# A two-layer gated cross-attention model: the first layer's down products in three passes of split operands

## The reference

```
x = x + tanh(g_xattn[0]) * LN(rs * softmax_attention(LN(x), ctx))        # layer 0, 16 heads
x = x + tanh(g_ffn[0]) * ((silu(h @ gate.T * gate_s) * (h @ up.T * up_s)) @ down.T) * down_s
x = x + tanh(g_xattn[1]) * ((linear_attention(q, ctx) * sigmoid(h @ Wg.T + bg)) @ Wo.T)
x = x + tanh(g_ffn[1]) * (top-2 of 16 experts (inner width 352) + one shared expert (704))
```

## Time and profile before

| | |
|---|---|
| median of 3 runs | 962.27 us (962.15 to 965.42) |
| the profiled execution, whole | 964.5 us |
| its span | 962.8 us |
| PE busy | 932.7 us, 97% of the span |
| DVE / ACT / POOL busy | 451.6 / 303.0 / 76.9 us |
| granted TensorE clock, mean | 0.995 |
| layer 0's down products (line 827) | 66.9 us busy |

### The profile page before, as it was taken

One profiled execution on the slowest core, in us unless ns is written; L12 is line 12 of the kernel. 1 busy time (PEld: TensorE's weight loads), 2 busy tenths in 40 slices (PEclk: granted clock), 3 DMA queues, 4 the chain that ended last, 5 costly groups with the idle time before them and its releaser, 6 DMA issues.

```text
span 962.8 us, 17950 instructions
## 1 busy us (share of the span) xinstructions
PE 932.7 (97%) x7523; PEld 720.6 (75%) x7524; DVE 451.6 (47%) x755; ACT 303.0 (31%) x477; POOL 76.9 (8%) x110
## 2 busy tenths in 40 slices
PE   5999999999999999989999999999999999999995
PEld 5878787878788888779999544888798766666554
DVE  6665545455455456873221154597665122222224
ACT  4633333332332334653211121335532222222210
POOL 0000000000000003000000000112006112122210
PEclk9999999999999999999999999999999999999998
DMA  8000010101011012044000300840503449787534
GB/s 338 10 27 34 1 34 1 34 1 34 5 74 34 1 35 78 2 154 175 1 1 1 131 1 0 318 182 1 181 1 131 156 170 329 285 290 241 210 123 166
DMA packets 26773, 96.04 MB, mean 100 GB/s; under 512 B 3282, under 2 KB 4306, under 8 KB 23634
## 3 DMA queue, kind: packets, MB, share of 16 engines
q1 hardware_dynamic: 20354, 72.69, 21.3%
q0 software_dynamic: 6352, 22.35, 6.2%
HBM read 76.37 MB, written 18.66 MB: 99 GB/s over the span
## 4 chain that ended last, share of the span: by engine, by line
PE 88%; DVE 6%; ACT 3%; DMA 2%; issue 1%; SPq 0%; POOL 0%; POOLq 0%; DVEq 0%; ACTq 0%
PE ps L563 18%; PE ps L564 17%; PE ps L565 17%; PE ps L991 10%; PE ps L827 7%; PE ps L1001 5%; PE ps L643 4%; PE ps L626 4%; PE ps L849 1%; PE ps L982 1%; DMA land_c<-in_ctx 1%; PE ps L665 1%; PE ps L963 1%; PE ps L612 1%; PE ps L1008 1%
## 5 line engine op out<-in xcount | busy, mean ns | idle before, releaser
L563 PE MATMUL ps<-arena_r 128*125 128x512 f32 (+1 forms) x416 | 163.8, 394 | 4.2 <-DVE arena_r L1357 4.2
L564 PE MATMUL ps<-arena_r 128*125 128x512 f32 (+1 forms) x416 | 157.0, 377 | 0.0
L565 PE MATMUL ps<-arena_r 128*125 128x512 f32 (+1 forms) x416 | 156.8, 377 | 0.0
L563 PE MATMUL ps<-hT,arena_r 128*128 128x448 f32 (+1 forms) x368 | 136.3, 370 | 2.4 <-DVE arena_r L1376 1.1
L565 PE MATMUL ps<-hT,arena_r 128*128 128x448 f32 (+1 forms) x368 | 134.4, 365 | 0.0
L564 PE MATMUL ps<-hT,arena_r 128*128 128x448 f32 (+1 forms) x368 | 134.4, 365 | 0.0
L991 PE MATMUL ps<-arena 128*128 x336 | 102.9, 459 | 0.0
L1062 ACT ACTIVATE arena<-arena,mbias,mscale 125x448 f32<-125x448 f32 x96 | 66.2, 752 | 102.0 <-DVE arena L1484 101.9
L563 PEld LDWEIGHTS ps<-arena_r 128*125 128x125 f32 (+1 forms) x416 | 78.0, 188 | 21.8 <-DVE arena_r L1357 4.6
L565 PEld LDWEIGHTS ps<-arena_r 128*125 128x125 f32 (+1 forms) x416 | 77.9, 187 | 13.8
L564 PEld LDWEIGHTS ps<-arena_r 128*125 128x125 f32 (+1 forms) x416 | 78.1, 188 | 10.7
(11 more groups left out here) (224 smaller groups left out, 1167.0 us busy)
## 6 DMA issues: line engine op xcount, KB each, us to landing
arena<-in_e SPq DMA_DIRECT2D x16, 1408.0 KB, 6.6
arena<-in_e SPq DMA_DIRECT2D x16, 512.0 KB, 7.4
sorted_rows<-arena POOLq DMA_DIRECT2D x1, 7453.0 KB, 34.0
land_c<-in_ctx SPq DMA_DIRECT2D x8, 752.0 KB, 4.2
arena<-sorted_rows POOLq DMA_DIRECT2D x21, 257.0 KB, 6.1
land_w<-in_gu SPq DMA_DIRECT2D x8, 512.0 KB, 5.3
arena<-token_rows SPq DMA_DIRECT2D x14, 256.0 KB, 4.5
arena<-in_e SPq DMA_DIRECT2D x16, 192.0 KB, 8.8
```

Of the source, the lines that this page charges most:

```text
L563: mm(into, a[0], w[0], start=i == 0, stop=False)
L564: mm(into, a[0], w[1], start=False, stop=False)
L565: last = mm(into, a[1], w[0], start=False, stop=i == len(operands) - 1)
```

## The change

1. **Down products.** `wd0` now lands in its own tensor `land_d` and is split into high and low halves in four pieces; `hidden` writes h in full into the landing area of the gate-up weights of the same m, from where ACT copies the high half and DVE takes the low half in place. `down_of_0` makes three passes, 33 matmuls per tile where there were 11, and waits per chunk for `h_low` and for the weight pieces.
2. **Later weights behind them.** `wg1` and `wo1` need regions that the down products now use: their loads wait for the last down product, `wg1` is split in two pieces between queries 2 to 4 and `wo1` after the attends. `wq1` has another region and waits for the last `hidden`.
3. **Zero fill.** It starts after the last `mix` of layer 0's attention, from a zero row of half the length (twice as many pieces); ACT waits for it ahead of the last layer norm.
4. **The end.** POOL's scatter copies the row numbers before it waits for DVE's copy into `yr`. Tile 6's shared product has no wait for DVE. DVE makes `shared_out` 4 and 5 ahead of the last additions. The odd tiles' last loads and stores are issued by ACT.

```diff
+        land_d = landing("land_d", A_WD, MC * D)
+        A_WDH = ([A_WH + i * D for i in range(4)] + [A_C + 5760 + i * D for i in range(3)] + [A_K + TOK]
+                 + [A_WH + 5120 + i * D for i in range(2)] + [A_WH + 2048])
+        wd0 = [halves(A_WDH[m], A_WD + m * D, land_d, D) for m in range(MC)]
-        h0 = [at(A_H0[m], TOK) for m in range(MC)]
+        h0 = [halves(A_H0[m], A_GU[m], land_c if 6 <= m < 9 else land_w, TOK) for m in range(MC)]
...
# SP
-            sp.wait_ge(ff_mm, MC)
+            sp.wait_ge(ff_h, MC)
             sp.dma_start(wq1[2], wq1_in).then_inc(wq1_ld, 16)
+            sp.wait_ge(y_mm, 2 * NT)
             sp.dma_start(wg1[2], wg1_in).then_inc(wg1_ld, 16)
             sp.dma_start(wo1[2], wo1_in).then_inc(wo1_ld, 16)
-            sp.wait_ge(y_mm, 2 * NT)
...
-            for t in range(NT):
+            for t in range(0, NT, 2):
                 sp.wait_ge(out_st, 1 + t)
                 sp.dma_start(out_t[t], x[:, t, :]).then_inc(x_ld, 16)
# PE
-            pe.wait_ge(wd0_ld, 16)
...
-                    if t == 0 and m == MC - 1:
-                        pe.wait_ge(ff_h, MC)
-                    last = mm(into, h0[m][:, t * P:(t + 1) * P], wd0[:, m, :], start=m == 0, stop=m == MC - 1)
+                    if t == 0:
+                        pe.wait_ge(h_low, m + 1)
+                        if m in (0, 4, 8, 10):
+                            pe.wait_ge(w_low, nth(("wd0a", "wd0b", "wd0c", "wd0d")[(0, 4, 8, 10).index(m)]))
+                    h = [half[:, t * P:(t + 1) * P] for half in h0[m][:2]]
+                    mm(into, h[0], wd0[m][0], start=m == 0, stop=False)
+                    mm(into, h[0], wd0[m][1], start=False, stop=False)
+                    last = mm(into, h[1], wd0[m][0], start=False, stop=m == MC - 1)
...
-                if first == 0 and t >= 2:
+                if first == 0 and 2 <= t < NT - 1:
                     pe.wait_ge(y_sv, 3 * NT + t - 1)
# ACT
                 fn(silu0[m % 2], ps[:, 4 * (1 - m % 2):4 * (1 - m % 2) + 2, 0:HALF], ACT.Silu,
                    scale=cols[:, 12 + m:13 + m]).then_inc(ff_silu, 1)
+                act.wait_ge(ff_h, m + 1)
+                fn(h0[m][0], h0[m][2], ACT.Copy).then_inc(h_high, 1)
+                if m == 3:
+                    down_high(0, 4).then_inc(w_high, 1)
...
+                if i in (2, 3):
+                    high("wg1" + "ab"[i - 2], wg1_part[i - 2], wg1_ld)
...
+            high("wo1", wo1, wo1_ld)
...
+            act.wait_ge(y_st, tiles * 16)
+            for t in range(1, NT, 2):
+                first = P + TOK + t * P
+                act.dma_start(back[t][1], y_dram[first:first + P, :]).then_inc(back_ld[t][1], 16)
+            for t in range(1, NT, 2):
+                act.wait_ge(out_st, 1 + t)
+                act.dma_start(out_t[t], x[:, t, :]).then_inc(x_ld, 16)
# DVE
+                if m >= 1:
+                    hidden_low(m - 1)
+                if m == 4:
+                    down_low("wd0a", 0, 4)
...
+                if m == 10:
+                    down_low("wd0c", 8, 10)
+                    down_low("wd0d", 10, 11)
...
+            hidden_low(MC - 1)
...
+                if i in (3, 4):
+                    low("wg1" + "ab"[i - 3], wg1_part[i - 3])
...
+            low("wo1", wo1)
             for i in range(3, 8):
                 gated_low(i)
...
+            for t in range(BEFORE, NT - 1):
+                shared_out(t)
             for t in range(NT):
-                if t >= BEFORE:
+                if t == NT - 1:
                     shared_out(t)
# POOL
-            pool.wait_ge(y_mm, 2 * NT)
+            pool.wait_ge(pv_mm, 4 * B)
             nc.gpsimd.memset(zero, 0.0).then_inc(zero_set, 1)
             pool.wait_ge(zero_set, 1)
-            pool.dma_start(xs_dram.rearrange("(t p) d -> p t d", p=P),
-                           zero.unsqueeze(1).broadcast_to([P, ROWS_MAX, ROW])).then_inc(filled, 16)
+            pool.dma_start(xs_dram.rearrange("(p t) (h d) -> p (t h) d", p=P, h=2),
+                           zero.unsqueeze(1).broadcast_to([P, ROWS_MAX * 2, ROW // 2])).then_inc(filled, 16)
...
-                pool.wait_ge(d_sv, n + 1)
+                pool.wait_ge(row_read, n + 1)
```

More of the change, by code:

```diff
@@ L372, in flamingo @@
         rank_sv = sem("rank_sv")
-        sh_copied = sem("sh_copied")
-        hsh_low = sem("hsh_low")
+        h_high = sem("h_high")
+        h_low = sem("h_low")
         dest_set = sem("dest_set")
@@ L413, in counts @@
                     for i in range(4)]
-        WEIGHTS = ("wk0a", "wk0b", "wv0", "wkv1a", "wkv1b", "gate", "wo0", "wq1", "wg1", "wo1", "sh2")
+        WEIGHTS = ("wk0a", "wk0b", "wv0", "wkv1a", "wkv1b", "gate", "wo0", "wd0a", "wd0b", "wd0c", "wd0d", "wq1", "wg1a",
+                   "wg1b", "wo1", "sh2")
         def nth(name):
@@ L445, in ln_tile @@
             return lnt0[:, n % 6, :] if n < NT else lnt1[:, n % NT % 4, :] if n < 2 * NT else lnt[:, n % 2, :]
+        out_t = out.rearrange("(t p) d -> t p d", p=P)
         @block.sync
@@ L541, in _ @@
                 sp.wait_ge(y_st, landed * 16)
-                for t in range(NT):
+                for t in range(0, NT, 1 + j):
                     first = P + j * TOK + t * P
                     sp.dma_start(back[t][j], y_dram[first:first + P, :]).then_inc(back_ld[t][j], 16)
-            out_t = out.rearrange("(t p) d -> t p d", p=P)
-            for t in range(NT):
+            for t in range(0, NT, 2):
                 sp.wait_ge(out_st, 1 + t)
@@ L878, in _ @@
                 query(6 + b)
-            pe.wait_ge(w_low, nth("wg1"))
+            pe.wait_ge(w_low, nth("wg1b"))
             for b in range(2, B):
@@ L955, in shared_part @@
                     if t == 0:
-                        pe.wait_ge(hsh_low, m + 1)
+                        pe.wait_ge(h_low, MC + m + 1)
                     h, w = ([half[0:z, t * P:(t + 1) * P] for half in hsh[m][:2]],
@@ L1206, in _, with down_high @@
             ln_save(NT + 6)
+            def down_high(first, end):
+                act.wait_ge(wd0_ld, 16)
+                words = (end - first) * D
+                return fn(at_r(A_WDH[first], words), land_d[1][:, first * D:end * D], ACT.Copy)
             for m in range(MC):
@@ L1224, in _ @@
                     high("wq1", wq1, wq1_ld)
-                if t == 2:
-                    high("wg1", wg1, wg1_ld)
-                if t == 3:
-                    high("wo1", wo1, wo1_ld)
                 if t >= 2:
@@ L1300, in _ @@
                 act.wait_ge(ff_h, MC + m + 1)
[L1301 to L1306 removed]
+                fn(hsh[m][0][0:size], hsh[m][2][0:size], ACT.Copy).then_inc(h_high, 1)
+            fn(sh2_kept[:, 0:4], sh2[0][:, 0:4].bitcast(F32), ACT.Copy).then_inc(h_high, 1)
+            fn(sh2_kept[0:96, 4:6], sh2[0][0:96, 4:6].bitcast(F32), ACT.Copy).then_inc(h_high, 1)
+            act.wait_ge(h_low, MC + 5)
+            fn(h4_kept[0:96], hsh[4][1][0:96, BEFORE * P:TOK].bitcast(F32), ACT.Copy).then_inc(h_high, 1)
             act.wait_ge(tables_set, 1)
@@ L1618, in hidden, with hidden_low, down_low @@
                                        silu[0:size], ALU.mult, ALU.mult).then_inc(ff_h, 1)
+            def hidden_low(m):
+                dve.wait_ge(h_high, m + 1)
+                v.tensor_tensor(h0[m][1], h0[m][2], h0[m][0].bitcast(F32), ALU.subtract).then_inc(h_low, 1)
+            def down_low(name, first, end):
+                dve.wait_ge(w_high, nth(name))
+                for m in range(first, end):
+                    last = v.tensor_tensor(wd0[m][1], wd0[m][2], wd0[m][0].bitcast(F32), ALU.subtract)
+                last.then_inc(w_low, 1)
             for m in range(MC):
@@ L1637, in _ @@
                     low("wq1", wq1)
-                if t == 2:
-                    low("wg1", wg1)
-                if t == 3:
-                    low("wo1", wo1)
                 if t >= 2:
@@ L1707, in shared_low @@
                 z = SH_CHUNKS[m]
-                dve.wait_ge(sh_copied, m + 1)
+                dve.wait_ge(h_high, MC + m + 1)
                 v.tensor_tensor(hsh[m][1][0:z], hsh[m][2][0:z], hsh[m][0][0:z].bitcast(F32), ALU.subtract
-                                ).then_inc(hsh_low, 1)
+                                ).then_inc(h_low, 1)
             dve.wait_ge(lg_mm, 3)
```

42 lines of the change are left out of this document (23 added, 19 removed).

## The result

The changed kernel takes 947.63 us in the median of 4 runs (945.65 to 949.65), the kernel before 963.85 us in the 4 runs beside it (962.15 to 965.8): a ratio of 0.9825 [0.9803, 0.9848]. Two more measurements of the changed kernel gave 0.9836 [0.98, 0.9871] and 0.9824 [0.9808, 0.9839]; in microseconds the three differences are 16.2, 16.2 and 17.7. The forecast was 944.6 us (941.5 to 950.0). The range held, the middle was 3 us too low. The profiled execution took 949.65 us, its span is 948.0 us, 14.8 less than before.

A forecast was written before the change was run, and what follows sets the result against it. The prediction took PE, busy for 97% of the span, as the bound, and at the program's end DMAs and waits. Its terms, -12.4 + 1.0 - 1.1 - 5.2 = -17.7 us, against a median of 962.27 gave 944.6 us (941.5 to 950.0).

The forecast's parts named there:

- Down products: Layer 0's down products: 33 records of 0.2324 us per tile, 7.67 us instead of 9.44, seven times: -12.4 us.
- Splits beside the feed-forward part: New ACT and DVE work during layer 0's feed-forward chunks fits beside PE, with 0.7 us margin at the last chunk: 0.
- Late `wg1`: Layer 1's queries: two splits of 1.15 us outlast DVE's 0.74 us waits, delaying DVE by about 0.9 us.
- Late `wo1`: Behind layer 1's last attend: its 2.29 us split and `gated_low(3)` end at 661.2, as do PE's gates; no more loss.
- Fill: Zero fill moved beside the gate-up and down weight loads: nobody waits, cost 0, at most 11 us.
- Scatters: Last two scatters: row numbers copied ahead shorten POOL's steps by 0.45 and 0.63 us: -1.1 us.
- End: Behind the last scatter's landing: without PE's wait transfers are the limit, 12.4 us instead of 17.6: -5.2 us.
- The end is held by latencies: Rival: last loads and stores land no faster, the end gives 2.5 + 1.1 instead of 6.3; 947.3 us, 12%.
- The splits hold up PE: Rival: in layer 1's attends the three moved splits count in full, +4.6 instead of +1.0; 948.2 us, 12%.
- DVE and POOL block each other: Rival: POOL's fill descriptor work stalls DVE's layer norms through the shared port, up to +3.8; 948.4 us, 4%.
- The fill starves the loads: Rival: the fill takes 68 us, the loads get nothing, PE loses 37 us on chunk 2's weights; 982 us, 3%.
- three passes are not faster: Rival: down products' 33 records stay at 0.429 us, 14.2 us per tile, +33 instead of -12.4; 990 us, 1%.

The follow-up runs named there:

- wg1_four: The changed kernel with `wg1` split in four pieces of 512 words behind the first four queries, instead of two of 1024: 948.56 us, ratio 0.9833.
- fill_late: The changed kernel with the zero fill, in its new short pieces, issued behind the last down product again: 951.81 us, ratio 0.9879.
- dve_late_wait: The changed kernel with DVE's `shared_out` 4 and 5 in their old place and PE's tile 6 waiting for DVE again: 952.5 us, ratio 0.987.
- sp_alone: The changed kernel with all seven last loads and all seven last stores issued by SP, none by ACT: 949.62 us, ratio 0.9848.
- wo1_ahead: The changed kernel with the split of `wo1` ahead of the last attend instead of behind it: 946.74 us, ratio 0.983.
- fill_halves: The kernel before with the zero fill at its old place, but in pieces of 257 words with each partition's rows side by side in DRAM: 965.61 us, one run.

## Why the prediction was right, and where its size was off

The sign, the likeliest case and the place of every term but one were right; the loss behind the last attend was forecast as nothing. No run has the down products alone. Their term, and the two of the late weights, are read from stretches of the profile that repeat from one execution to the next: the first is 54.70 or 54.72 us in all eleven profiles with the new products and 67.85 in the three with the old ones. In the profile, term by term:

- **Down products**, forecast -12.4: from the silu of chunk 10 to DVE's step behind the last tile 67.85 us before and 54.72 after, **-13.1**. The products run at 0.2286 us a record over the first three tiles (537.24 to 559.87 are 99 of them), a little under the 0.2324 of the earlier trace rows, and over 231 records that makes up the difference.
- **Splits beside the feed-forward part**, forecast 0: right, with 0.6 us of margin (543.5 against 544.13) where 0.7 was worked out.
- **Late `wg1`**, forecast 0.9 in the queries: **+0.9**, and so in all nine profiles of kernels with these two pieces (21.0 to 21.1 us instead of 20.2). `wg1_four` shows that the 0.74 us of the earlier trace rows were there to be filled.
- **Late `wo1`**, forecast "no more loss, but no margin": **+1.9**. This is the step that failed. The prediction set DVE's end only against PE's last gate, and on that its sum was good: with a `gated_low` of 0.62 us DVE would have been done at 648.6, when PE's gates were. It left out POOL, whose four multiplies stand between the last attend product and the last `gated_low`. In the kernel before they ended at 657.42 + 4.79 = 662.2, behind PE's gates, and 2.0 us ahead of DVE's first `output_of_1` step, for which 1.2 us are enough in the changed kernel; so POOL had some 0.8 us to spare. The split took more: POOL's first multiply lasted until 649.07, 1.0 us beyond the split's end at 648.07, and the others followed 1.5 us apart beside DVE's `gated_low`. Four at 1.2 us from 645.95 would have been done at 650.8; they were done at 653.55, and 2.8 us less the 0.8 are the 1.9 within 0.1.
- **Fill**, forecast 0: right for the early place beside the feed-forward loads, although it took 57.3 us and not 41. "Its removal gains nothing" held for the place before; `fill_late` shows that in the changed kernel this fill would have cost 3.4 us at the old place. That its place and the other parts hang together the prediction didn't see.
- **Scatters**, forecast -1.1: POOL's steps got shorter by just that (1.98 to 1.51 us and 2.15 to 1.51 us from the start of DVE's copy to the transfer), but the last scatter but one now lands after 4.34 us instead of 3.54: **-0.3** in all. It landed in 3.54 and 3.63 us in the two profiles with the old end and in 3.84 to 5.45 in the profiles with the new one. Why is open.
- **End**, forecast -5.2: **-5.1**, but put down to the wait alone. It is 4.0 for the pair of PE's wait and DVE's order (`dve_late_wait`) and 1.2 for the second issuer (`sp_alone`), of which the prediction said that it saves SP's time alone and to which it gave nothing. That the whole came out within 0.1 us is in part luck. The Trainium skill, "DMA: Bandwidth & Descriptors", section "Issuing engines are not separate DMA queues", says that several issuers save only the time it takes to initiate the DMAs. The trace agrees: full engines moved 410 GB/s with one issuer and 405 with two, and the gain is in the time of issue.

The sum of these is -15.7 us (forecast -17.7), and the medians differ by 16.2. The profile's 14.8 has two items more that aren't the change's: the feed-forward part started 1.0 earlier and its chunks went at the slower of two paces (+1.8). Of the 3.0 us by which the time was missed, 1.5 are this smaller difference and the other half is the yardstick: the forecast stood on a median of 962.27, and the kernel before measured 962.95 to 964.63 in the four sets that followed.

Three rivals have times nearer to 947.63 than the forecast's, so the time alone decides nothing between them. "The end is held by latencies" (947.3) is refuted: it had 2.5 us behind the last scatter's landing, and 5.1 came. "The splits hold up PE" (948.2) was right by half: 2.8 of its 4.6 us are there, but 1.9 of them through POOL, not by splits that count in full. "DVE and POOL block each other" (948.4) was right as a mechanism and put in the wrong place: at the fill's issue (2.73 us instead of 1.89) nothing was lost, and PE's wait of the earlier trace rows is 3.13 us as before; behind the last attend it cost 1.9 us. Here the rule of the Trainium skill, "SBUF — State Buffer", section "SBUF: two separate sides", bears on the trace. It holds for a DVE instruction with two inputs in SBUF beside one of GpSimd that reads SBUF: whichever starts first keeps the other out until it is through. `wo1`'s split and `gated_low` are such instructions. The trace agrees: the split started first (645.79) and kept its 2.28 us, POOL's first multiply took 3.12 us and ended 1.0 us behind it, and `gated_low`, issued at 647.99, ended 0.5 us behind that multiply. The four `gated_low` beside POOL took 1.13 to 1.57 us instead of 0.62, and by `wo1_ahead` POOL gets 2.0 of its 2.8 us back when the split is taken away. "The fill starves the loads" and "three passes are not faster" are refuted.

## What to carry to other kernels

When work is moved to a new place, list every engine that has work on the path there, the helper with a few instructions too, and ask which of them slows down beside the newcomer; here it was GpSimd, which the page shows busy 8% of the span. An edit that looks worth nothing may be paying for another edit of the same change, so take parts out of the whole one by one and in pairs: the fill's place shows its price only in the changed kernel, and the two halves of the end's coupling show theirs only together. And filling an engine's small waits with pieces just their size works (0.69 us in a wait of 0.74), whereas pieces of twice the size stand out by their excess.

## What the runs showed of the hardware that was not expected

- A fill of 7.45 MB from SBUF to DRAM in pieces of half the length (257 words) and with each partition's rows side by side in DRAM took 48.3 us where the old form (514 words) took 34.0 at the same place; beside other loads it took 53.1 (`fill_late`) and 56.7 to 58.6 us. While it ran, full DMA engines moved 254 to 294 GB/s in most stretches of 10 us (207 and 312 at the outside), not 403. Whether the length or the order in DRAM does it is open.
- PE stood idle for 0.50 to 1.74 us with nothing to wait for, in runs of small 32x112 products, while the DMA engines were full (`fill_late`; one gap of 0.74 us in `fill_halves`). The page lists a DMA queue of kind "instruction" (56 packets, 0.92 MB); that PE's instructions came late through it fits, but is not shown.
- Dense three-pass products went at one of two paces per execution, 9.73 or 9.92 us a chunk, at a granted clock of 1.00 in both, with either kernel.
- A DVE instruction with two SBUF operands beside GpSimd's multiplies took 1.1 to 1.6 us instead of 0.6, and GpSimd's first, issued behind a DVE instruction of 2.28 us, took 3.12 instead of 1.46 us.
